# Attention in pairs of heads on one core: 64-row tiles side by side, units of two banks, shift rows by DMA, and the output chain moved into the next batch

## The reference

```
x = x + attn(layernorm(x))
x = x + moe(layernorm(x))

# attn, per batch and head (16 heads, head size 16, T = 512):
qkv = x @ W_attn + b_attn            # q and k are then rotated by an angle that depends on the head
att = (q @ k.T) / sqrt(16)           # 512 x 512, masked above the diagonal
att = softmax(att)
y   = att @ v                        # 512 x 16
out = y @ W_proj + b_proj
```

## Time and profile before

| what | value |
|---|---|
| median of three runs | 1977.81 us |
| profiled execution | 1974.22 us, span 1972.5 us, mean granted clock 0.978 |
| TensorE busy over the span | 1812.9 us |
| VectorE, ScalarE, GpSimd busy | 1190.6, 987.3, 825.0 us |
| attention | first scores at 62.07 us, last at 933 us, first matmul of the experts at 990.91 us |

### The profile page before, as it was taken

The page is one execution under the profiler, slowest core; times in us unless marked ns, Lnnn a source line. Parts: engine busy times, 40 slices in busy tenths (PEclk is TensorE's granted clock), DMA queues, the critical chain, the costliest instruction groups (busy, mean ns, idle before and its releaser), DMA issues. The chain is left out here.

```text
span 1972.5 us, 45605 instructions
## 1 busy us (share of the span) xinstructions
PE 1812.9 (92%) x13586; PEld 1124.6 (57%) x13587; DVE 1190.6 (60%) x2539; ACT 987.3 (50%) x1577; POOL 825.0 (42%) x1186
## 2 busy tenths in 40 slices
PE   1699999999999999999489899999999999999997
PEld 1345555555555555554266566665666666666664
DVE  4567777777777777777436777773333333333332
ACT  1377777776767777767333322453333333333332
POOL 2033333333333333334120177624555555555554
PEclk9799999999999999999689999999999999999999
DMA  1212222122222222211154564322333333333332
GB/s 53 74 54 74 71 65 60 59 68 72 74 72 72 72 64 72 61 44 60 34 189 128 170 193 116 89 78 54 59 59 56 57 58 59 59 58 56 57 58 43
DMA packets 155397, 146.32 MB, mean 74 GB/s; under 512 B 32753, under 2 KB 145905, under 8 KB 155250
## 3 DMA queue, kind: packets, MB, share of 16 engines
q1 hardware_dynamic: 125042, 108.65, 18.3%
q0 software_dynamic: 30208, 35.81, 11.6%
HBM read 75.65 MB, written 43.52 MB: 60 GB/s over the span
## 5 line engine op out<-in xcount | busy, mean ns | idle before, releaser
L794 ACT ACTIVATE prob<-bank,exp_scale 128x512 f32<-128x512 f32 x640 | 429.4, 687 | 191.1 <-PE bank L1571 184.8
L619 POOL TENSOR_SCALAR_AFFINE_SELECT prob<-prob 128x256 f32<-128x256 f32 (+1 forms) x640 | 239.4, 378 | 478.9 <-ACT prob L794 478.0
L1058 DVE TENSOR_REDUCE mx<-bank 128x1 f32<-128x512 f32 (+2 forms) x768 | 361.2, 505 | 118.8 <-PE bank L1543 118.6
L1466 PE MATMUL bank<-wbuf,xt 128*128 x1632 | 374.4, 379 | 1.0 <-DVE xt L1354 1.0
L731 POOL DMA_INDIRECT out_x<-ysb,tok_rows x136 | 215.4, 1583 | 240.2 <-ACT ysb L918 197.7
L1527 PE MATMUL bank<-k_op,q_op 96*128 96x512 f16 (+3 forms) x1024 | 250.6, 306 | 29.9 <-DVE mx L1067 12.3
L1359 DVE TENSOR_TENSOR htl<-bank,hth 128x512 f16<-128x512 f32 x200 | 138.0, 690 | 224.6 <-ACT hth L882 219.0
L1368 DVE SCALAR_TENSOR_TENSOR hb<-bank,h_s,sg 128x512 f32<-128x512 f32 x200 | 149.9, 749 | 202.4 <-PE bank L1466 202.0
L1571 PE MATMUL bank<-q_op,k_op 128*128 128x512 f16 (+3 forms) x1024 | 243.5, 299 | 12.7 <-ACT prob L794 12.0
L1466 PEld LDWEIGHTS bank<-wbuf,xt 128*128 128x128 f16 x1632 | 159.6, 98 | 163.1 <-issue 1.1
L918 ACT ACTIVATE ysb<-bank,row_w 128x256 f32<-128x256 f32 x136 | 64.5, 474 | 310.0 <-PE bank L1466 310.0
(11 more groups left out here) (209 smaller groups left out, 2747.3 us busy)
## 6 DMA issues: line engine op xcount, KB each, us to landing
x_in<-in_L_attn_x SPq DMA_DIRECT2D x16, 512.0 KB, 4.4
q_op<-qkh SPq DMA_DIRECT2D x256, 32.0 KB, 1.9
k_op<-qkh SPq DMA_DIRECT2D x512, 16.0 KB, 1.8
xres<-in_L_attn_x SPq DMA_DIRECT2D x16, 512.0 KB, 4.9
x_d<-x SPq DMA_DIRECT2D x32, 256.0 KB, 2.1
xhl_d<-xhl SPq DMA_DIRECT2D x32, 256.0 KB, 2.4
xrow<-xhl_d SPq DMA_DIRECT2D x64, 128.0 KB
wbuf<-xhl_d SPq DMA_DIRECT2D x16, 512.0 KB, 4.7
```

What stands on the lines that cost most here:

```text
L619: nc.gpsimd.affine_select(out=v, in_=v, compare_op=ALU.is_ge, fill=0.0, base=0, pattern=pat, channel_multiplier=-1).then_inc(S["sel_done"], 1)
L794: nc.scalar.activation(prob[:, half, u, :], ps_t[u % 2][:], ACT.Exp, scale=exp_scale[:]).then_inc(S["exp_done"], 1)
L1058: return nc.vector.tensor_reduce(out, src[:, lo:lo + n], AX_X, ALU.max)
L1466: last = nc.tensor.matmul(out, a, m, start=(i == 0), stop=(i == n - 1))
```

## The change

- **Operands.** Two heads share one index of `q_op` and `k_op`: an even head lies in rows 0 to 47, an odd one in rows 64 to 111. Each head's q and k are copied in three thirds of 16 rows: 24 copies per group in place of 18, all on SP. `k_op` is filled with the shift constant once, and `q_op` is no longer cleared.
- **Units.** A unit is a pair of heads in two banks (`pair_s`, `pair_t`), so `UN` is 5 and no longer 10. The two heads' matmuls stand next to each other in two tiles of 64 rows. The mask is added by four matmuls of 64 rows, two of them with a shifted identity and mask (`ident_x`, `mask_x`). There is one such pair of banks for the scores and one for the shifted scores, so unit u waits for the maxima, or the exponential, of unit u-1.
- **Reads of two banks.** One VectorE reduction or one ScalarE exponential reads both banks. The scale of the exponential comes from a register.
- **Shift rows.** ScalarE writes the scaled maxima to `m_row` and then issues four DMAs on its own queue that put one row each into `q_op`.
- **Order.** All tables of slots are new; `LAG` is 7 of 5-slot groups instead of 13 of 10-slot groups. Parts of the output chain of a batch move to the batch after the next, which adds a `body(NB + 1)`. The second half of a V projection and of an output projection has a slot of its own.

```
-    UN = 10
-    LOADS = 18 * 16
+    UN = 5
+    LOADS = 24 * 16
+    MROWS = 4 * 16
+    KR = 48
...
-        LAG = 13
-        MAXIMA, M_ROWS = 2, 2
-        MIX, O_OUT = (2, 4, 5, 6), 7
+        LAG, MAXIMA, M_ROWS, O_OUT = 7, 0, 0, 2
+        MIX = (0, 2, 2, 2)
...
+            body(NB + 1, 1, cur=False, prev=False, prev2=True, nxt=False, nxt2=False)
...
                 r0 = 64 * (g % 2)
-                for quad, (qs, ks) in enumerate(((qkh, qkh), (qkh, qkl), (qkl, qkh))):
-                    for t in range(2):
-                        sp.dma_start(q_op[32 * quad:32 * quad + 32, 2 * g + t, :],
-                                     qs[r0 + 32 * t:r0 + 32 * t + 32, 2 * j, :]).then_inc(ops_in[g], 16)
+                for third, (qs, ks) in enumerate(((qkh, qkh), (qkh, qkl), (qkl, qkh))):
                     for h in range(GH):
-                        row = 32 * quad + HD * (h % 2)
-                        sp.dma_start(k_op[row:row + HD, GH * g + h, :],
-                                     ks[r0 + HD * h:r0 + HD * (h + 1), 2 * j + 1, :]).then_inc(ops_in[g], 16)
+                        row = 64 * (h % 2) + HD * third
+                        pair = 2 * g + h // 2
+                        head = slice(r0 + HD * h, r0 + HD * (h + 1))
+                        sp.dma_start(q_op[row:row + HD, pair, :], qs[head, 2 * j, :]).then_inc(ops_in[g], 16)
+                        sp.dma_start(k_op[row:row + HD, pair, :], ks[head, 2 * j + 1, :]).then_inc(ops_in[g], 16)
...
-            nc.gpsimd.memset(q_op[:], 0.0).then_inc(S["pool_const"], 1)
-            pool.wait_ge(S["k_zeroed"], 1)
-            pool.wait_ge(S["pool_const"], 4)
-
-            k_sel = k_op[96:128].rearrange("p (g h) n -> p g h n", h=GH)
-            nc.gpsimd.affine_select(out=k_sel, in_=k_sel, compare_op=ALU.not_equal, fill=-SHIFT_UNIT, base=0,
...
+            def shift_rows(G, g, half):
+
+                act.wait_ge(S["m_in"], G)
+                if some(G - 2):
+                    act.wait_ge(S["mrow_in"], MROWS * (G - 2))
+                nc.scalar.activation(m_row[:, half], ps_m[0:GH, :], ACT.Copy, scale=1.0 / SHIFT_UNIT
+                                     ).then_inc(S["m_done"], 1)
+                act.wait_ge(S["m_done"], G)
+                for h in range(GH):
+                    row = 64 * (h % 2) + KR
+                    act.dma_start(q_op[row:row + 1, 2 * g + h // 2, :], m_row[h:h + 1, half]
+                                  ).then_inc(S["mrow_in"], 16)
...
-                if some(UN * G + u - 1):
-                    pe.wait_ge(S["max_done"], UN * G + u - 1)
...
+                if some(UN * G + u):
+                    pe.wait_ge(S["max_done"], UN * G + u)
+
+                def mm(pair, q, lo, start):
+                    for a in range(2):
+                        nc.tensor.matmul(ps_s[a][:, lo:lo + P * (q + 1)],
+                                         q_op[64 * a:64 * a + KR, pair, P * q:P * (q + 1)],
+                                         k_op[64 * a:64 * a + KR, pair, 0:P * (q + 1)], start=start, stop=False)
...
+                if u < 2:
+                    last = nc.vector.tensor_reduce(dst[:, 3, 2 * u:2 * u + 2], pair_s[:], AX_X, ALU.max)
...
+                nc.scalar.activation(prob[:, half, u].rearrange("p a n -> p (a n)"),
+                                     pair_t[:].rearrange("p a n -> p (a n)"), ACT.Exp,
+                                     scale=exp_by).then_inc(S["exp_done"], 1)
```

More of the change, by code:

```diff
@@ L263, in build @@
[L263 to L275, removed]
@@ new lines, in build, with heads_here, halves_here @@
+        STEPS = (X1, X1_STATS, X1_VARIANCE, RSTD_B, ROWS, HIGH, LOW)
+        def heads_here(at, table, b, prev, prev2):
+            return [(j, b - 1 - head_lag(table, j)) for j in range(len(table))
+                    if table[j] == at and (prev2 if head_lag(table, j) else prev)]
+        def halves_here(at, table, b, prev, prev2):
+            before = STEPS[:[table is t for t in STEPS].index(True) + 1]
+            return [(j, b - 1 - half_lag(j, *before)) for j in range(2)
+                    if table[j] == at and (prev2 if half_lag(j, *before) else prev)]
@@ L1169, in body @@
                     for s in range(UN):
+                        for i in range(4):
+                            if cur and prev and (g, s) == QK_LOW[i] and QK_LOW[i] < QK[i]:
+                                qk_low(b, i)
                         if cur:
@@ L1199, in body @@
[L1199 to L1206 removed]
+                        for q, bp in heads_here((g, s), DIVIDE, b, prev, prev2):
+                            divide(bp, q)
@@ new lines, in body @@
+                        for j, bp in halves_here((g, s), X1, b, prev, prev2):
+                            residual(bp, j)
+                        for j, bp in halves_here((g, s), X1_STATS, b, prev, prev2):
+                            residual_stats(bp, j)
+                        for j, bp in halves_here((g, s), X1_VARIANCE, b, prev, prev2):
+                            residual_variance(bp, j)
+                        for j, bp in halves_here((g, s), ROWS, b, prev, prev2):
+                            rows(bp, j)
@@ L1207, in body @@
+                        for j, bp in halves_here((g, s), LOW, b, prev, prev2):
+                            low(bp, j)
+                        if not cur and prev and (g, s) == PREP_MAX:
                             prepare_maxima()
-                        if not cur and (g, s) == PREP_SCALE:
+                        if not cur and prev and (g, s) == PREP_SCALE:
                             prepare_scales()
-                        if not cur and (g, s) in PREP_LOW:
+                        if not cur and prev and (g, s) in PREP_LOW:
@@ L1211, in body @@
                             prepare_low(PREP_LOW.index((g, s)))
-                if not cur:
-                    residual_variance(b - 1, 1)
-                    rows(b - 1, 1)
-                    low(b - 1, 1)
             batches(dve, body, link, DVE_LINKS)
@@ L1511, in prologue @@
                 for j in range(2):
-                    project_v(0, j, V_BANK[j])
+                    for t in range(2):
+                        project_v(0, j, t, V_BANK[j])
                 for i in range(2, 4):
@@ new lines, in scores @@
+                for i in range(2):
+                    for a in range(2):
+                        rows = slice(64 * a, 64 * a + 64)
+                        eye, tri = (ident_b, mask) if a == i else (ident_x, mask_x)
+                        sel = ps_s[a].rearrange("p (s n) -> p s n", n=P)[:, blocks, :]
+                        last = nc.tensor.matmul(sel, eye[rows], tri[rows].unsqueeze(1).broadcast_to(
+                            [64, sel.shape[1], P]), start=False, stop=(i == 1))
+                last.then_inc(S["s_in"], 1)
```

349 lines of the change are left out of this document (169 added, 180 removed).

## The result

| | before | after |
|---|---|---|
| median | 1977.46 us (1975.88 to 1981.45) | 2208.03 us (2205.99 to 2212.99) |
| ratio | 1 | 1.1164, interval 1.1144 to 1.1184 |
| profiled execution: span, clock | 1972.5 us, 0.978 | 2204.3 us, 0.908 |
| one batch in the steady part | 54.3 us | 68.35 us |
| first matmul of the experts | 990.91 us | 1222.23 us |

A forecast was written before the change was run, and what follows sets the result against it. The prediction took TensorE, by a small margin over SyncE's queue, to bound the kernel before. SyncE's added issuing (+253), less waits (20.0) and prologue (7.7), plus tail (2), gave +227 us: 2205 us, range 2170 to 2290.

The forecast's parts named there:

- SyncE's queue at 98%, TensorE with a small margin: Attention before the change: SyncE issued for 846.6 of 866.6 us; TensorE, nearly full too, set the pace.
- SyncE's queue as the bound of the changed kernel: Attention: 68.8 us of SyncE per batch against 54.3; 17 us per group against some 11 us of TensorE work.
- 384 more loads at 0.66 us: Attention, SyncE's queue: 1536 loads instead of 1152, +253 us of issuing (243 to 263).
- Prologue: Before attention: clearing `q_op` and the select over `k_op` go, so first rstd moves from 25.8 to about 18, -7.7 us.
- Tail: Last group to experts: scores start with the last load, -2 us; moved output chain, +4 us (0 to 12); together +2.
- The sum: Whole program: SyncE's stream of 1100 us ends at 1141.3, +225 us; with the tail +227, median 2205 us.
- The work on the other engines: Attention: TensorE, VectorE, ScalarE and single-bank-pair hand-overs take about 11 us per group, hidden under SyncE's 17 us.
- The clock: Attention: TensorE's idling may lower its clock, making a group 15 us, still under 17: no cost while SyncE bounds.
- 250 us of TensorE's waits for loads: First scores of each group: TensorE waits for DMAs into `q_op` or `k_op`, 4 to 6 us each, 250 us or more.
- Two tiles side by side: Scores and shifted scores: two heads' matmuls run together, halving each, 2.2 us of TensorE per group saved.
- Loads are not the bound: Rival, attention: issue time shrinks below 0.509 us, TensorE sets the pace, about 1863 us; chance 0.11.
- ScalarE's DMAs hold up SyncE's: Rival, attention: both queues share the issue cost, 28 issues per group, +169 us, about 2374 us; chance 0.11.

The follow-up runs named there:

- e1: Kernel before the change, with q's copies cut in two, so 24 loads per group instead of 18: ratio to before 1.102, 16.95 us per group.
- b12: Kernel before the change, with the last third of the operands loaded in the first batch only, 12 loads per group instead of 18: ratio to before 0.9997.
- g3: g2 with its two shift-row DMAs behind the group's first exponential instead of ahead of it: ratio to before 0.9810, 13.06 us per group.
- e2: Changed kernel, last third of q and k not loaded after the first batch, 16 loads per group instead of 24: ratio to before 1.0935, 16.79 us per group.
- e3: Changed kernel, last third not loaded for two of four heads after the first batch, 20 loads per group: ratio to before 1.0952, 16.75 us per group.
- g1: Changed kernel, whole computation, q and k rows of a head in one DMA, 12 loads per group instead of 24: ratio to before 1.0994, 16.80 us per group.
- g2: g1 with two shift-row DMAs instead of four, still ahead of the group's first exponential: ratio to before 1.0140, 14.06 us per group.
- e4: Changed kernel without ScalarE's four shift-row DMAs per group, all 24 loads kept: ratio to before 1.1023, 17.08 us per group.
- e5: Changed kernel with the cuts of e2 and e4 together, 16 loads and no shift-row DMAs per group: ratio to before 0.9772, 12.78 us per group.
- e6: Changed kernel, GpSimd issuing the last third's eight loads per group from the second batch on, SyncE 16: ratio to before 1.0962, 16.71 us per group.

## Why the prediction was right, and where it was not

- **SyncE's queue at 98%, TensorE with a small margin.** Right, and shown by e1 (six more loads per group: +217 us) and b12 (six fewer: nothing).
- **SyncE's queue as the bound of the changed kernel.** Right, but only by 0.3 us per group (17.1 against 16.8), not by the 6 that I had given it.
- **384 more loads at 0.66 us.** The stream took 1132.9 - 43.8 = 1089 us against 1100 forecast, so the added loads cost (1089 - 847)/384 = 0.63 us each, the lower bound. Waits of the queue: none, as said. Batch: 68.35 against 68.8 us.
- **Prologue.** GpSimd's first rstd came at 19.26 in place of 25.82, and the first load 5.6 us earlier, not 7.7. From the select of the mask to rstd it is 2.3 us now and was 11.3, as forecast; but that select itself comes 2.4 us later (16.94 against 14.50), since the chain ahead of it started later and holds two memsets more.

```profile
16.94 0.29 POOL L602 TENSOR_SCALAR_AFFINE_SELECT mask<-mask 128x128 bf16<-128x128 bf16 x1
...
19.26 1.06 POOL L618 TENSOR_TENSOR rstd<-mv,neghalf 128x4 f32<-128x4 f32 x1 [0.30 <-POOLq L612]
```

- **Tail.** Mis-sized, +14.4 us in place of +2. The last group's scores started 2.65 us after the last issue, as forecast (though the row names the maxima, not a load), but from there to the experts it took 86.65 us in place of 70.9, and I had given it 4 more. The clock in that stretch was 0.64 (0.73 before).

```profile
1135.58 0.39 PE L1547 MATMUL pair_s<-k_op,q_op 48*128 48x512 f16 x2 [1.19 <-DVE mx L1093]
...
1222.23 0.58 PE L1747 MATMUL pair_t<-ident_h,xrow 128*128 128x128 f16 x4 [10.98 <-DMA xrow<-xhl_d]
```

  From the last group's shift rows to the experts g3 takes 63.6 us, the changed kernel 67.3 and the kernel before 55.0, so 3.7 us of the excess go with what g3 changed, and 8.6 us stay with the moved output chain or the single pair of banks; which of these two, no run tells. The remaining 3.4 us lie between the last group's scores and its shift rows (19.3 us in place of 15.9), and stay open too.
- **The sum.** The stream came out 11 us shorter and the stage started 2 us later; the tail was 12 us longer. The three errors cancel to 3 us, so the closeness of 2205 to 2208 is luck.
- **The work on the other engines "at 11 us per group", "hidden".** This is the step that failed, and the time did not show it: ScalarE's DMA issues were priced as ScalarE's work and not as a wait in the chain. With SyncE's loads out of the way the rest takes 16.8 us (e2, e3, g1), 0.3 us less than the loads. I had the price of ScalarE's issues right (2 to 2.8 us; 2.54 measured), but added it to ScalarE's busy time, where it does not matter, in place of the chain. Ahead of an exponential on which TensorE waits, it costs 16.79 - 12.78 = 4.0 us per group. The other 1.8 us of the error (11 against 12.8) no run takes apart.
- **The clock: "nothing".** Right only for as long as SyncE was the bound, as I had written. By the busy times it is 1.7 of the 2.7 us between g1 and g2.
- **250 us of TensorE's waits for loads.** Wrong: 9.4 us of its own waits named a load of `k_op`, and 38.9 us came by the way round over `xres`, which the prediction had not seen. TensorE was itself nearly as late as the loads. In e4, without ScalarE's issues, waits for loads came up (86.6 us in 760).
- **Two tiles side by side.** Right: two matmuls of 512 columns started together at 490.48 and the next ones 0.23 us later, the time of one. TensorE's busy time per group fell from 12.9 to 11.4 us (e5) at clock 0.97; with the clock taken out (11.4 x 0.97 = 11.1, an estimate) by 1.8 us, and not 2.2.
- **Rivals.** "Loads are not the bound" (1863 us) had its condition wrong: with the loads out of the way the kernel stays at 1.09, and needs ScalarE's issues out of the way as well. "ScalarE's DMAs hold up SyncE's" is refuted by e4: 17.08 us per group with or without them, SyncE 0.63 us from start to start in both. That agrees with "DMA: Bandwidth & Descriptors", section Issuing engines are not separate DMA queues, in the Trainium skill, as the prediction read it.

What stays open: no run changed the hold and the clock apart from each other, so that the clock's 1.7 us is read from busy times and not from a run of its own. A second pair of banks, in place of moving the DMAs, was not tried.

## What to carry to other kernels

A queue that only issues DMAs is a worker like any engine: count its issues times their price before an edit adds some, because it fills without showing as busy, and its lateness can appear under other names (a wait for GpSimd's `select`, or ScalarE's for `qkh`). A DMA issued by a compute engine costs what stands behind it: put it behind the instruction on which the others wait, and make one DMA of two where strides allow. When one bound is removed and nothing happens, do not drop the theory before the second suspect is removed with it; e2 and e4 alone looked like refutations (0.3 us per group and nothing), and together gave 4.3 us of 17.1.

## What the runs showed of the hardware

- A DMA from SBUF to SBUF costs its queue the same for one block of 16 rows (589 ns) as for two (593 ns median in g1, twice the bytes), and on ScalarE one of two rows cost 567 ns (g3) and one of one row 611. ScalarE's issues beside them left SyncE's price as it was (0.63 us from start to start in the changed kernel and in e4), and ScalarE's median was 611 ns beside a full SyncE queue and beside one with 12 loads per group (g1).
- TensorE ran at half clock (granted 0.50, the level of 1.2 GHz) behind a wait of 3.4 us in g1. In g1 such waits, 2.4 us on average, came 47 times between 100 and 860 us, and the mean clock of this stretch was 0.85; in g2, with waits of 1.3 us at the same place, it was 0.97.
- GpSimd issued eight such loads per group at 0.48 us of busy time each, with no loss of time per group (16.71 us in e6, 16.79 in e2), although GpSimd also worked off the selects on which `mix` waits.
